# The bias of the experts' reconstruction moves from VectorE's subtraction to ScalarE's square

## The chip, the cores and the metric

One Trainium2 chip, of which the kernel uses one core. The metric is the device time of one execution in microseconds (us); lower is better. A core has five engines that run their own queues in order: TensorE (PE in the rows; its weight loads are PEld), VectorE (DVE), ScalarE (ACT), GpSimd (POOL) and SyncE (SP, here the queue that issues the DMAs). They meet through semaphores.

## The reference

A batch of 64 sequences of 128 tokens, 256 wide, goes through two layers: cross attention and a quantised feed-forward net, then cross attention and a feed-forward net with a selected adapter. The last one matters here:

```python
base = einsum('btd,do->bto', x, W_base) + b_base
h = relu(einsum('btd,edh->ebth', x, Wd1) + bd1[:, None, None, :])
recon = einsum('ebth,ehd->ebtd', h, Wd2) + bd2[:, None, None, :]
losses = mean((recon - x[None]) ** 2, axis=(2, 3))
idx = argmin(losses, axis=0)
a = relu(einsum('btd,bdr->btr', x, Wa_down[idx]) + ba_down[idx][:, None, :])
return base + einsum('btr,bro->bto', a, Wa_up[idx]) + ba_up[idx][:, None, :]
```

Each of 8 experts reconstructs the sequence; the one with the smallest squared error lends its adapter. Only the comparison of the losses is used, so their sum stands for their mean.

## The kernel before, in words

Two sequences are one pair `p`, 32 pairs in all; a pair's activations are 256 columns, `T`, held transposed with the width of 256 on partitions in two halves `k`. The work of a pair is cut into steps, and each step has a slot: the step with offset `o` runs for pair `p` at `t = o + 16 p`. Each engine has one loop over `t`, in which an order written out by hand says what it does in each slot. So steps of five pairs are interleaved on every engine, and after the fill one period of 16 slots finishes one pair. An engine that waits for a semaphore holds all that stands behind it in its loop.

The steps that the change touches or that stand around it:

- TensorE, `reconstruct(p, m)` (L1261): the reconstructions of experts 2m and 2m+1, each a PSUM bank of 512 columns (two halves of the width, 256 columns each).
- VectorE, `differences(p, e)` (L942): for each half, (reconstruction + `bd2s`) - `xT3` into the SBUF tile `dif`, 256 columns an instruction; four such tiles serve the eight experts in turn.
- ScalarE, `squares(p, e)` (L683): for each of the two sequences, the square of 2 x 128 columns with its sum into a column of `acc`. Such a call leaves two instructions in the trace, an ACTIVATE and an ACTIVATION_READ_ACCUMULATOR.
- TensorE, `losses(p)` (L1269): a matmul with ones sums `acc` over the partitions; `choose` on VectorE finds the expert, and SP's `gather` fetches its adapter.
- ScalarE, `exps(l, p, j)` (L639): the exponential of 512 columns of scores. All scores for it go through one PSUM bank, `X`: `scores_t` (L1192) may write group j+1 only when the exponential of group j is done.
- ScalarE, `copy_xT(2, p)` (L616): copies the transposed activations out of PSUM, and TensorE's `queries(1, p)` (L1154) reads the copy. `high(1, 0, p)` (L630) then takes the queries out of PSUM, `values1` (L647) the values, and `relus` (L663), the two `hd_relus` (L675) and `a_relus` (L690) are activations with a bias of one number per partition.

In ScalarE's loop the squares stand among those. In the order of one period, with the pairs left out: exps(1,1), squares 0, exps(1,2), squares 1, values1, exps(1,3), squares 2, squares 3, exps(1,4), copy_xT(2), high(1,0), exps(1,5), squares 4, exps(1,6), copy_xT(1), squares 5, squares 6, exps(1,7), squares 7, relus 0, exps(0,0). In TensorE's loop, queries(1) stands between reconstruct 2 and scores(0,3); losses stands behind mix(1,1), and behind losses come scores(0,7), count and scores_t(0,1), which needs exps(0,0) done.

Of the kernel before, what the change touches and what calls it, by code (L numbers as in the profile page):

```python
# [8 lines left out]
F32 = mybir.dt.float32  # L9
# [4 lines left out]
ALU = mybir.AluOpType  # L14
ACT = mybir.ActivationFunctionType
# [3 lines left out]
P = 128  # L19
B = 64  # L20
D = 256
KD = D // P
# [4 lines left out]
E = 8  # L27
R = 64
PB = 2
NP = B // PB  # L30
T = PB * P
# [81 lines left out]
def build(nc, x, lens, mask, mask_t, wq0, bq0, wk0, bk0, wv0, bv0, wo0, bo0, w1t, b1, w2t, b2,  # L113
          wq1, wk1, wv1, wo1, w_base, wd1, bd1, wd2, bd2, adapters, ctx_in, out):
    with ExitStack() as ctx:
        def sb(name, shape, dt):
            return ctx.enter_context(nc.sbuf_tensor(name, shape, dt))
# [4 lines left out]
        def sem(name):  # L122
            return ctx.enter_context(nc.semaphore(name))

        def signal(name, per=1):
            return Signal(sem(name), per)
# [20 lines left out]
        bd2s = sb("bd2s", [P, E, KD], F32)  # L147
        ident = sb("ident", [P, P], F32)
        onesb = sb("onesb", [P, P], BF16)
        ones = sb("ones", [P, 1], F32)  # L150
# [17 lines left out]
        xT3 = sb("xT3", [P, 2, KD, T], F32)  # L168
# [29 lines left out]
        hhl = sb("hhl", [P, 2, KF, T], F16)  # L198
        hd = sb("hd", [P, E // 2, T], F32)
        dif = sb("dif", [P, 4, KD, T], F32)  # L200
        acc = sb("acc", [P, E, PB], F32)
        lneg = sb("lneg", [1, PB, E], F32)
        lmax = sb("lmax", [1, PB, 8], F32)
        lidx = sb("lidx", [1, PB, 8], U32)
# [11 lines left out]
        bank = {name: DB[k] for name, k in place.items()}  # L216
# [19 lines left out]
        loss_ready = signal("loss_ready")  # L236
# [11 lines left out]
        squared = signal("squared", E * PB)  # L248
# [17 lines left out]
        v0_copied = signal("v0_copied")  # L266
        x_low = signal("x_low")
        h_low = signal("h_low", KF // 2)
        diffed = signal("diffed", E * KD)
        loss_out = signal("loss_out")  # L270
        best_loss = signal("best_loss", PB)
        expert_found = signal("expert_found", PB)
# [327 lines left out]
        def _(act):  # L600
# [76 lines left out]

            def squares(p, e):
                loss_ready.done(act, p - 1)
                diffed.done(act, p, 2 * e + 1)  # L680
                for b in range(PB):
                    blk = dif[:, e % 4, :, b * P:b * P + P]
                    nc.scalar.activation(blk, blk, ACT.Square, accum_out=acc[:, e, b:b + 1]).then_inc(squared.sem, 1)  # L683

            def a_relus(p):
                down_ready.done(act, p)
# [7 lines left out]
            for t in range(FIRST, END):  # L694
                for p in at(t, 64):
                    squares(p, 0)
                for p in at(t, 48):
                    exps(1, p, 2)
                for p in at(t, 65):
                    squares(p, 1)  # L700
# [3 lines left out]
                for p in at(t, 65):  # L704
                    squares(p, 2)
                    squares(p, 3)
# [71 lines left out]
        def _(dve):  # L778
# [154 lines left out]
            def differences(p, e):  # L933
                rec_ready.done(dve, p, e // 2)
                if p == 0 and e == 0:
                    dve.wait_ge(w_late, 16 * len(LATE))
                if e >= 4:
                    squared.done(dve, p, 2 * (e - 4) + 1)
                else:
                    squared.done(dve, p - 1, 2 * (e + 4) + 1)  # L940
                for k in range(KD):
                    nc.vector.scalar_tensor_tensor(  # L942
                        out=dif[:, e % 4, k], in0=bank[f"rec{e}"][:, k * T:k * T + T],
                        scalar=bd2s[:, e, k:k + 1], in1=xT3[:, p % 2, k], op0=ALU.add,
                        op1=ALU.subtract).then_inc(diffed.sem, 1)

            def choose(p):
                loss_ready.done(dve, p)
# [27 lines left out]
            for t in range(FIRST, END):  # L976
                for p in at(t, 16):
                    turn_out(0, p, 1)
                for p in at(t, 64):
                    differences(p, 1)  # L980
                for p in at(t, 16):
                    scale_out(0, p, 1)
                for p in at(t, 64):
                    differences(p, 2)
                for p in at(t, 0):
                    maximum(0, p, 0)
                for p in at(t, 65):
                    differences(p, 3)
# [110 lines left out]
        def _(pe):  # L1099
            holder = {}  # L1100

            def claim(what, consumer, p, n=None):

                if what in holder:
                    last, pair, event = holder[what]
                    last.done(pe, pair, event)
                holder[what] = (consumer, p, n)

            def dense(name, consumer, p, n=None):
                claim(place[name], consumer, p, n)  # L1110
                return bank[name]

            def warm(dst, *what):

                for _ in range(WARM.get(what, 0)):
                    nc.tensor.matmul(dst[:, 0:P], ident[:], ident[:], start=True, stop=True)
# [136 lines left out]
                ins.then_inc(hd_ready.sem, 1)  # L1253

            def reconstruct(p, m):
                dst = [dense(f"rec{2 * m + s}", diffed, p, 4 * m + 2 * s + 1) for s in range(2)]
                hd_relu.done(pe, p, m)
                for k in range(KD):
                    for s in range(2):
                        half = slice(R * s, R * s + R)  # L1260
                        ins = nc.tensor.matmul(dst[s][:, k * T:k * T + T], wd2s[half, m, k * P:k * P + P], hd[half, m],  # L1261
                                               start=True, stop=True)
                ins.then_inc(rec_ready.sem, 1)

            def losses(p):
                dst = dense("loss", loss_out, p)
                warm(dst, "losses", p)
                squared.done(pe, p)
                nc.tensor.matmul(dst[0:1, 0:E * PB], ones[:], acc[:].rearrange("p e b -> p (e b)"), start=True, stop=True)\  # L1269
                    .then_inc(loss_ready.sem, 1)  # L1270

            def down(p):
                dst = dense("down", a_relu, p)
# [22 lines left out]
            for t in range(FIRST, END):  # L1296
                for p in at(t, 64):
                    reconstruct(p, 1)
# [18 lines left out]
                for p in at(t, 67):  # L1317
                    reconstruct(p, 2)
# [12 lines left out]
                for p in at(t, 68):  # L1331
                    reconstruct(p, 3)
# [16 lines left out]
                for p in at(t, 71):  # L1349
                    losses(p)  # L1350
# [126 lines left out]
```

## Time and profile before

| | us |
|---|---|
| median of 3 runs (1646.77 to 1651.4) | 1646.82 |
| the profiled execution, its own time | 1648.25 |
| its span, which all rows below are in | 1646.4 |
| busy: TensorE matmuls | 1566.2 (95%) |
| busy: VectorE | 1307.6 (79%) |
| busy: GpSimd | 1100.4 (67%) |
| busy: ScalarE | 893.3 (54%) |

The chain of work that ended last is 80% TensorE, 7% VectorE and 1% ScalarE. A busy share is a mean over fill, steady part and end; what a change is worth has to be read in the steady part and in the end apart. In a timeline row, the first number is the start in us from the span's start, the second the time taken (of all merged instructions where there is "x8"), and brackets hold the engine's idle time before the row and what ended it.

### The profile page before, as it was taken

The numbers are of one execution on the slowest core, as the hardware profiler recorded it, in microseconds if no ns is written. First come the engines' busy times: TensorE is split into PE (matmuls) and PEld (weight loads), VectorE is DVE, ScalarE is ACT, GpSimd is POOL, SyncE is SP. The second block draws the span as 40 slices with busy tenths as digits, with TensorE's granted clock in tenths as the row PEclk, the third lists the DMA queues.
The fourth block names the chain that finished last, engine by engine and source line by source line (L and its number), as shares of the span: only waits on it lengthen the run. The fifth ranks groups of instructions, "written<-read, shape, count | busy, mean of one in ns | idle before, by whom it ended". The sixth has DMA issues, their size and how long they took to land.

```text
span 1646.4 us, 44358 instructions
## 1 busy us (share of the span) xinstructions
PE 1566.2 (95%) x15358; PEld 1303.5 (79%) x15358; DVE 1307.6 (79%) x5141; ACT 893.3 (54%) x2465; POOL 1100.4 (67%) x1197
## 2 busy tenths in 40 slices
PE   5788999999999999999999999999999999999887
PEld 4666888888888888888888888888888888887666
DVE  7457888898888888988888889888888898887552
ACT  0134565665555656655556566655565665555542
POOL 4576777766776777667777776667777766766300
PEclk7889999999999999999999999999999999999988
DMA  8446666555656665555566655565666465553311
GB/s 202 79 85 95 95 102 106 92 99 95 99 102 108 103 107 93 102 92 98 102 108 104 105 94 101 95 96 100 108 111 99 90 102 94 98 82 50 56 36 33
DMA packets 286482, 157.28 MB, mean 96 GB/s; under 512 B 39089, under 2 KB 281906, under 8 KB 286258
## 3 DMA queue, kind: packets, MB, share of 16 engines
q1 hardware_dynamic: 286258, 154.44, 54.8%
q8 instruction: 123, 2.02, 0.6%
q14 instruction: 101, 0.83, 0.2%
HBM read 111.36 MB, written 41.96 MB: 93 GB/s over the span
## 4 chain that ended last, share of the span: by engine, by line
PE 80%; DVE 7%; issue 4%; DMA 4%; POOL 3%; SPq 1%; ACT 1%; DVEq 0%; POOLq 0%; ACTq 0%
PE psD L1261 7%; PE psS L1179 7%; PE psD L1251 6%; PE psV L1206 6%; PE psD L1162 6%; PE psX L1192 6%; PE psD L1219 6%; PE psD L1154 6%; PE psD L1240 6%; PE psD L1144 6%; PE psD L1232 6%; PE psD L1288 4%; PE psD L1124 3%; DMA qs<-scr 3%; PE psD L1290 2%
## 5 line engine op out<-in xcount | busy, mean ns | idle before, releaser
L532 POOL TENSOR_TENSOR pT<-pT,keep 128x512 f32<-128x512 f32 x256 | 321.2, 1271 | 87.6 <-ACT pT L639 87.5
L639 ACT ACTIVATE pT<-psX 128x512 f32<-128x512 f32 x512 | 305.2, 596 | 110.5 <-PE psX L1192 104.8
L517 POOL TENSOR_SCALAR xn<-xr,mv,rstd 128x256 f32<-128x256 f32 x256 | 312.0, 1226 | 10.4
L491 POOL TENSOR_SCALAR veps<-mv 128x2 f32<-128x2 f32 x128 | 29.3, 229 | 355.8 <-DVE mv L811 353.5
L876 DVE CUSTOM_DVE_ANT_0 dump<-psS,bias 128x128 bf16<-128x128 f32 x1024 | 233.8, 282 | 19.8 <-PE psS L1179 18.1
L1179 PE MATMUL psS<-ks,qs 65*128 65x128 f16 x2048 | 200.6, 221 | 24.9 <-DMA qs<-scr 22.9
L942 DVE SCALAR_TENSOR_TENSOR dif<-psD,bd2s,xT 128x256 f32<-128x256 f32 x512 | 213.6, 465 | 12.8 <-PE psD L1261 12.7
L683 ACT ACTIVATE dif<-dif 128x256 f32<-128x256 f32 x512 | 207.6, 414 | 25.6 <-DVE dif L942 22.9
L1192 PE MATMUL psX<-qs,ks 67*128 67x128 f16 x2048 | 199.8, 219 | 11.3 <-ACT pT L639 10.2
L1179 PEld LDWEIGHTS psS<-ks,qs 65*128 65x128 f16 x2048 | 145.8, 98 | 73.1 <-issue 27.3
L868 DVE TENSOR_REDUCE mx<-psS 128x4 f32<-128x512 f32 x256 | 169.4, 671 | 24.2 <-PE psS L1179 24.1
L1192 PEld LDWEIGHTS psX<-qs,ks 67*128 67x128 f16 x2048 | 139.9, 97 | 45.9 <-ACT pT L639 18.8
L616 ACT ACTIVATE xT<-psD 128x512 f32<-128x512 f32 x96 | 57.2, 596 | 198.5 <-PE psD L1124 198.5
L537 POOL TENSOR_TENSOR hhl<-work,hhl 128x512 f16<-128x512 f32 x128 | 147.6, 1160 | 18.9 <-ACT hhl L669 16.1
L1206 PE MATMUL psV<-pT,v 128*32 128x128 f32 x4096 | 140.9, 279 | 10.3 <-POOL pT L532 4.6
L630 ACT ACTIVATE packed<-psD 128x512 f16<-128x512 f32 x96 | 57.4, 598 | 171.6 <-PE psD L1154 75.9
L1261 PE MATMUL psD<-hd,wd2s 64*128 64x256 f32 x1024 | 146.0, 404 | 2.6 <-DVE dif L942 2.6
L1232 PE MATMUL psD<-xs,w1q 128*128 128x256 f16 x1024 | 134.4, 274 | 1.2 <-DVE xs L924 1.2
L663 ACT ACTIVATE work<-psD,b1s 128x256 f32<-128x256 f32 x256 | 108.0, 478 | 48.1 <-PE psD L1232 43.7
L1206 PEld LDWEIGHTS psV<-pT,v 128*32 128x32 f32 x4096 | 106.1, 111 | 30.8 <-issue 12.1
L1162 PE MATMUL psD<-wv,ctxT 128*128 128x256 f32 x512 | 130.4, 399 | 0.0
L1154 PE MATMUL psD<-xT,wq 128*128 128x256 f32 x512 | 126.2, 389 | 2.1 <-ACT xT L616 2.1
(102 smaller groups left out, 3218.0 us busy)
## 6 DMA issues: line engine op xcount, KB each, us to landing
scr<-packed SPq DMA_DIRECT2D x128, 256.0 KB, 2.9
ks<-scr SPq DMA_DIRECT2D x256, 128.0 KB, 5.3
qs<-scr SPq DMA_DIRECT2D x256, 128.0 KB, 4.4
adapter<-in_adapters SPq DMA_DIRECT2D x64, 192.5 KB, 2.6
xr<-in_x SPq DMA_DIRECT2D x32, 256.0 KB, 2.8
ctxT<-in_ctx SPq DMA_DIRECT2D x32, 256.0 KB, 2.8
qs<-mrows SPq DMA_DIRECT2D x512, 2.0 KB
out_y<-xr SPq DMA_DIRECT2D x32, 256.0 KB, 5.3
```

The costliest lines, as they stand in the source:

```text
L517: nc.gpsimd.tensor_scalar(xn[:, XN[s], b], xr[:, p % NX, b], mv[:, s, b, 0:1], rstd[:, s, b:b + 1], ALU.subtract, ALU.mult).then_inc(norme ...
L532: nc.gpsimd.tensor_tensor(blk, blk, keep[:, p % 2, j // 4].unsqueeze(1).to_broadcast([P, 4, P]), ALU.mult).then_inc(masked.sem, 1)
L639: nc.scalar.activation(pT[:, j], X[:], ACT.Exp, scale=SCALE).then_inc(exp_done[l].sem, 1)
L876: ins = nc.vector.tensor_tensor_reduce(out=dump[:, a], in0=S[:, a * P:a * P + P], in1=bias0[:, p % 2, b], scale=1.0, scalar=-3e38, op0=ALU ...
L942: nc.vector.scalar_tensor_tensor(out=dif[:, e % 4, k], in0=bank[f"rec{e}"][:, k * T:k * T + T], scalar=bd2s[:, e, k:k + 1], in1=xT3[:, p % ...
L1154: ins = nc.tensor.matmul(dst[:, m * T:m * T + T], wq[l][:, k, m * P:m * P + P], src[:, k], start=(k == 0), stop=(k == KD - 1))
L1162: ins = nc.tensor.matmul(dst[:, b * D:b * D + D], ctxT[:, p % NC, k * T + b * P:k * T + b * P + P], wv[l][:, k], start=(k == 0), stop=(k = ...
L1179: ins = nc.tensor.matmul(S[:, a * P:a * P + P], qs[0:MASK_ROW + 1, r, h, t0:t0 + P], ks[0:MASK_ROW + 1, r, h, t0:t0 + P], start=True, stop ...
L1192: ins = nc.tensor.matmul(X[:, a * P:a * P + P], ks[0:ROWS, r, h, t0:t0 + P], qs[0:ROWS, r, h, t0:t0 + P], start=True, stop=True)
L1206: ins = nc.tensor.matmul(V[32 * a:32 * a + 32, n * P:n * P + P], v2[l][:, b, n // 2 * UH + 2 * a + n % 2], pT[:, 4 * b + n, a * P:a * P + ...
L1232: ins = nc.tensor.matmul(dst[:, m * T:m * T + T], w1q[:, k, f0:f0 + P], xs16[:, part, k], start=(n == 0), stop=(n == 2 * KD - 1))
L1261: ins = nc.tensor.matmul(dst[s][:, k * T:k * T + T], wd2s[half, m, k * P:k * P + P], hd[half, m], start=True, stop=True)
```

## The change

The bias leaves the subtraction. `differences` becomes one subtraction over the whole bank, 512 columns. `squares` passes the bias to the activation, which adds it before the square. As the bias differs between the two halves of the width, one activation can cover only one half: four activations of 128 columns for an expert, where there were two of 256. `acc` becomes twice as large, and `losses` sums it with two accumulating matmuls. The semaphore `diffed` counts experts rather than halves.

```diff
-        acc = sb("acc", [P, E, PB], F32)
+        acc = sb("acc", [P, KD, E, PB], F32)
@@ squares (ScalarE)
-                diffed.done(act, p, 2 * e + 1)
+                diffed.done(act, p, e)
                 for b in range(PB):
-                    blk = dif[:, e % 4, :, b * P:b * P + P]
-                    nc.scalar.activation(blk, blk, ACT.Square, accum_out=acc[:, e, b:b + 1]).then_inc(squared.sem, 1)
+                    for k in range(KD):
+                        blk = dif[:, e % 4, k, b * P:b * P + P]
+                        ins = nc.scalar.activation(blk, blk, ACT.Square, bias=bd2s[:, e, k:k + 1],
+                                                   accum_out=acc[:, k, e, b:b + 1])
+                    ins.then_inc(squared.sem, 1)
@@ differences (VectorE)
-                for k in range(KD):
-                    nc.vector.scalar_tensor_tensor(
-                        out=dif[:, e % 4, k], in0=bank[f"rec{e}"][:, k * T:k * T + T],
-                        scalar=bd2s[:, e, k:k + 1], in1=xT3[:, p % 2, k], op0=ALU.add,
-                        op1=ALU.subtract).then_inc(diffed.sem, 1)
+                nc.vector.tensor_tensor(dif[:, e % 4].rearrange("p k t -> p (k t)"), bank[f"rec{e}"][:],
+                                        xT3[:, p % 2].rearrange("p k t -> p (k t)"), ALU.subtract)\
+                    .then_inc(diffed.sem, 1)
@@ reconstruct (TensorE)
-                dst = [dense(f"rec{2 * m + s}", diffed, p, 4 * m + 2 * s + 1) for s in range(2)]
+                dst = [dense(f"rec{2 * m + s}", diffed, p, 2 * m + s) for s in range(2)]
@@ losses (TensorE)
-                nc.tensor.matmul(dst[0:1, 0:E * PB], ones[:], acc[:].rearrange("p e b -> p (e b)"), start=True, stop=True)\
-                    .then_inc(loss_ready.sem, 1)
+                for k in range(KD):
+                    ins = nc.tensor.matmul(dst[0:1, 0:E * PB], ones[:], acc[:, k].rearrange("p e b -> p (e b)"),
+                                           start=(k == 0), stop=(k == KD - 1))
+                ins.then_inc(loss_ready.sem, 1)
```

## Rows read from the trace of the kernel before

**Rows 1.** Busy time by stretch; columns: length, busy (instructions) by engine, granted clock, DMA.

```profile
600.00:1000.00 400.00, 397.96 (x4005) 331.97 (x4004) 337.54 (x1341) 233.83 (x650) 289.29 (x313) 1.00 0.60 102
```

**Rows 2.** Waits of TensorE's matmuls, 250 to 1400 us; columns: total, times, longest.

```profile
PE psS L1179 <- DMA qs<-scr: 1.1, 3, 0.4
PE psD L1219 <- DVE attT L911: 1.1, 2, 0.8
PE psD L1288 <- ACT aT L690: 0.3, 1, 0.3
```

**Rows 3.** Groups of instructions, shapes apart: busy us, mean ns, idle before.

```profile
L942 DVE SCALAR_TENSOR_TENSOR dif<-psD,bd2s,xT 128x256 f32<-128x256 f32 x512 | 213.6, 465 | 12.8 <-PE psD L1261 12.7
L965 DVE TENSOR_TENSOR xr<-psD,xr 128x512 f32<-128x512 f32 x32 | 22.1, 692 | 71.0 <-PE psD L1290 71.0
L683 ACT ACTIVATE dif<-dif 128x256 f32<-128x256 f32 x512 | 207.6, 414 | 25.6 <-DVE dif L942 22.9
L683 ACT ACTIVATION_READ_ACCUMULATOR dif<-dif 128x1 f32 x512 | 101.0, 197 | 0.0
L675 ACT ACTIVATE hd<-psD,bd1s 128x256 f32<-128x256 f32 x128 | 53.8, 471 | 113.1 <-PE psD L1251 113.1
L647 ACT ACTIVATE v<-psD 128x256 f32<-128x256 f32 x64 | 21.1, 381 | 14.2 <-PE psD L1162 14.2
L690 ACT ACTIVATE aT<-psD,adapter 64x128 f32<-64x128 f32 x64 | 23.0, 360 | 30.2 <-PE psD L1278 29.4
```

**Rows 4.** Timeline of ScalarE through one steady period, in part.

```profile
806.34 0.60 ACT L639 ACTIVATE pT<-psX 128x512 f32<-128x512 f32 x1 [1.53 <-PE psX L1192]
806.83 0.41 ACT L683 ACTIVATE dif<-dif 128x256 f32<-128x256 f32 x1
...
807.23 0.41 ACT L683 ACTIVATE dif<-dif 128x256 f32<-128x256 f32 x1
...
809.74 0.66 ACT L647 ACTIVATE v<-psD 128x256 f32<-128x256 f32 x2 [0.39 <-PE psD L1162]
...
810.28 0.60 ACT L639 ACTIVATE pT<-psX 128x512 f32<-128x512 f32 x1
...
814.02 0.60 ACT L616 ACTIVATE xT<-psD 128x512 f32<-128x512 f32 x1 [1.00 <-PE psD L1124]
...
817.01 0.60 ACT L630 ACTIVATE packed<-psD 128x512 f16<-128x512 f32 x1 [2.39 <-PE psD L1154]
...
824.91 0.84 ACT L663 ACTIVATE work<-psD,b1s 128x256 f32<-128x256 f32 x2 [1.01 <-PE psD L1232]
825.64 0.60 ACT L639 ACTIVATE pT<-psX 128x512 f32<-128x512 f32 x1
```

**Rows 5.** Timeline of TensorE through the same period, in part.

```profile
814.98 1.99 PE L1154 MATMUL psD<-xT,wq 128*128 128x256 f32 x8
...
825.93 0.20 PE L1269 MATMUL psD<-acc,ones 128*1 128x16 f32 x2
826.07 0.40 PE L1179 MATMUL psS<-ks,qs 65*128 65x128 f16 x4
...
826.41 0.39 PE L1192 MATMUL psX<-qs,ks 67*128 67x128 f16 x4
826.64 1.95 PE L1144 MATMUL psD<-ctxT,wk 128*128 128x256 f32 x8
```

**Rows 6.** Timeline of the end: pairs 29 and 30, then the last.

```profile
1556.94 0.60 ACT L639 ACTIVATE pT<-psX 128x512 f32<-128x512 f32 x1
...
1557.60 0.40 PE L1192 MATMUL psX<-qs,ks 67*128 67x128 f16 x4 [1.01 <-ACT pT L639]
1557.93 1.08 PE L1206 MATMUL psV<-pT,v 128*32 128x128 f32 x32
...
1601.83 1.94 PE L1206 MATMUL psV<-pT,v 128*32 128x128 f32 x32 [2.16 <-ACT pT L639]
...
1633.22 0.21 PE L1269 MATMUL psD<-acc,ones 128*1 128x16 f32 x2
```

More of the change, by code:

```diff
@@ L268, in build @@
         h_low = signal("h_low", KF // 2)
-        diffed = signal("diffed", E * KD)
+        diffed = signal("diffed", E)
         loss_out = signal("loss_out")
```

## The prediction, made before the changed kernel was seen

> **What bounds the kernel now.** I read the busy time by stretch first. In 400 us of the steady part TensorE's matmuls are busy for 397.96 us at a granted clock of 1.00, which is the 2.4 GHz level; VectorE is busy for 337.54 and ScalarE for 233.83 [rows 1]. Then TensorE's waits: between 250 and 1400 us there are three rows, 2.5 us together, and one of them, 0.3 us, names ScalarE [rows 2]. So TensorE sets the period (46.84 us: the exponential that starts at 806.34 comes again at 853.18). A faster VectorE is worth nothing there, and a slower ScalarE costs nothing until one of its steps comes later than TensorE wants it. The shares don't say where that is, as ScalarE's 58% is not spread evenly. The timelines of ScalarE and TensorE through one period do, laid side by side.
>
> **The subtraction.** Two instructions of 256 columns, 213.6 / 256 = 0.834 us an expert, become one of 512. The nearest row, a subtraction's twin (PSUM and SBUF in, SBUF out, f32, 512 columns), takes 0.692 us [rows 3]. VectorE gets 0.14 us an expert back, 1.1 us a period, 36 us in all. TensorE waits for it almost nowhere in the steady part [rows 2], so I count it at nothing there.
>
> **The squares.** Now an expert is two activations, 0.40 us from start to start, the read of the accumulator included [rows 4]: 0.80 us. It becomes four, of half the columns and with a bias. Half the columns: the bias activations of 256 and of 128 columns take 471 and 360 ns, so 128 columns fewer save 0.11 us. The bias: activations of 256 columns out of PSUM take 471 ns with and 381 ns without one, so it costs 0.09 us [rows 3]. Start to start that gives 0.40 - 0.11 + 0.09 = 0.38 us, 1.52 us an expert, 0.72 more than now. The bounds: if the bias hides under the instruction before it, 0.29; if nothing overlaps, as between the two activations of L690 (0.74 us for the two of them in the timeline, so 0.38 from start to start), 0.38 and about 0.09 for the read's slot, 0.47. I take 0.38, since both of its terms are differences of rows that are otherwise alike, and L690 runs on 64 partitions with another operand.
>
> The Trainium skill bears on that choice (ScalarE: Activation LUTs, What ACT_TABLE_LOAD costs): an activation with a pointer operand costs 280 ns and 0.833 ns a column, each pointer some 93 ns of it, and neighbours overlap by 93 ns. The trace's 0.09 for the bias agrees. By that rule a half would be 387 ns less the overlap, with the read's slot near 0.385, which speaks for the middle and against 0.47. The same page's rules for kernel authors would leave an add to VectorE.
>
> **Where ScalarE comes late, first place.** It starts exps(1,1) at 806.34 after waiting for TensorE. From there to copy_xT(2) it has four exponentials at 0.49 (806.34 to 806.83), values1 at 0.54 (809.74 to 810.28) and four experts' squares [rows 4]. Now that is 1.96 + 0.54 + 3.20 = 5.70, and gaps fill the rest up to 814.02. With the change it is 1.96 + 0.54 + 6.08 = 8.58 us without a gap: the copy starts at 814.92 and ends at 815.52. Release takes 0.05 (the exponential of 1556.94 ends at 1557.54, the matmul starts at 1557.60 [rows 6]). TensorE wants to start queries(1) at 814.98 [rows 5] and starts at 815.57: 0.59 us late. On the way the two-deep places hold: X for exps(1,3) is free by 811.5, wanted at 812.0.
>
> **Second place.** high(1,0) waits for the queries, so it starts at 817.01 + 0.59 = 817.60. Behind it come five activations of 512 columns at 0.49 (itself, exps(1,5), exps(1,6), copy_xT(1), exps(1,7)), four experts at 1.52, relus 0 at 0.73 (824.91 to 825.64) and exps(0,0) at 0.60 [rows 4]: 817.60 + 2.45 + 6.08 + 0.73 + 0.60 = 827.46, with the release 827.51. TensorE wants scores_t(0,1) at 826.41 [rows 5], 827.00 after the first delay: 0.51 more. After a true wait the next group follows a group of scores at 0.33 instead of 0.23 (1557.60 to 1557.93 against 826.41 to 826.64) [rows 5, 6]: 0.10. After that ScalarE waits for TensorE again several times, so nothing is carried into the next period.
>
> **The loss.** One more matmul a pair, two records: 825.93 to 826.07, 0.14 us [rows 5]. It stands just ahead of the second stall and hides in it. If that stall is absent, it costs 0.14 x 32 = 4.5 us.
>
> **The ends.** First place: pairs 0 to 29 have a queries(1) two pairs on, 30 x 0.59 = 17.7 us. Second: pairs 0 to 27 have an exps(0,0) four pairs on, 28 x 0.61 = 17.1 us. In the squares of pairs 29 and 30 little other TensorE work is left, and mix(1,1) waits for ScalarE already (2.16 us for pair 30 [rows 6]). Laying 1.52 us an expert through the same order: for pair 29 exps(1,3) ends 1.0 later, queries(1) starts 2.05 later, mix(1,1) about 3.8 later, of which 0.59 is counted: 3.2 more. For pair 30, seven experts stand ahead of exps(1,7), partly in gaps: 3.7. The last pair's eight squares now end behind the warm-up matmuls that stand ahead of the loss at 1633.22 [rows 6]: from a first square at 1621.7, 8 x 1.52 ends at 1633.9, with the second loss matmul 1.0 later. Together 7.9 us.
>
> **The sum.** 17.7 + 17.1 + 3.2 + 3.7 + 1.0 = 42.7 us on the profiled execution's own 1648.25 (span 1646.4 and 1.85 around it): 1691. The median of the runs lies 1.4 lower, so 1690. It hangs on the start-to-start time of a half: 16 halves stand ahead of each place, so 0.01 us on it is 0.32 us a period, some 10 us in all. The two places stop stalling at 0.345 (16 x 0.345 = 5.52 against 3.20 and 2.3 of slack). From 0.345 to 0.41 the time goes from about 1656 to 1720.
>
> **Rivals.** (a) ScalarE's slack covers the squares, not slower: the bias hides, a half costs 0.29 from start to start, below the 0.345 from which it decides. Then no place stalls; the loss matmul costs 2 to 4.5 us, the ends lose about 1 and get 1 back from VectorE: 1647 to 1652, 1650. For it: 54% busy. Against it: the 0.09 between two rows of one shape. (b) No overlap in such short activations: 0.47. That is 0.09 x 16 x 2 = 2.9 us a period more, 84 us, and 5 at the ends: 1780. For it: L690's pair. Against it: the squares overlap today although a read stands between them, and so do L675's two activations (0.84 for two of 471 ns). (c) VectorE turns out to pace the period, and its 1.1 us a period come back: 1647 - 36 = 1611 at most. Against it: rows 2. (d) The change doesn't do what it says: a subtraction over 512 columns isn't faster than two of 256. It would alter nothing, as long as VectorE stays off the path.
>
> **Chances.** The forecast (two stalls a period, a half between 0.345 and 0.42) 0.76, with (d) in it; (a) 0.11; (b) 0.08; (c) 0.05. A measurement of this kernel can tell 0.3%, 5 us, from no change. Faster 0.05, all of (c). Same 0.10, nearly all of (a). Slower 0.85. The range of 1656 to 1722 takes in the forecast from the point where it starts to stall to a half of 0.41, and leaves out most of (a), (b) and (c).
>
> **What would show it.** In the profile after, L683 should have 1024 activations near 0.40 us, 0.38 from start to start (two of them with their reads 0.76), and as many reads, and ScalarE should be busy for about 190 us more. TensorE's waits should have two new rows in every period: L1154 on ACT xT L616, about 30 times near 0.6 us, and L1192 on ACT pT L639, about 28 times near 0.5. The period should be 48.0 us. VectorE should lose 36 us of busy time. If the period stays 46.9, the half is cheaper than 0.345, and if it is near 51, nothing overlaps. The forecast's weakest step is the 0.38; next to it that nothing of a late period is carried over, since a third place could then stall.

## The result and the profile after

The changed kernel takes 1685.78 us (median of 4 runs, 1681.19 to 1687.65) against 1648.16 for the kernel before in the same comparison. The ratio is 1.0233, 95% interval 1.021 to 1.0256: 2.3% slower, 37.6 us. The forecast was 1690, 43 us slower, in a range of 1656 to 1722. The profiled execution after took 1687.24 us, its span is 1685.4; before, 1648.25 and 1646.4. So the two spans, on which the following rests, are 39.0 us apart. One kernel's executions scatter: 30 of the kernel before, in a later comparison, took 1641.6 to 1651.4 us, the shorter ones at a mean granted clock of 0.983 and the longer at 0.978. So a few us in a single profile can be chance.

The busy time by stretch of the kernel after, in the stretch of [rows 1] (columns as there):

```profile
600.00:1000.00 400.00, 392.65 (x3939) 326.21 (x3938) 323.60 (x1251) 272.24 (x894) 288.31 (x312) 1.00 0.58 99
```

TensorE is idle for 7.4 us in 400, where it was idle for 2.0, at the same granted clock of 1.00. The waits of its matmuls between 250 and 1400 us, which answer [rows 2], say why:

```profile
PE psD L1155 <- ACT xT L616: 13.1, 24, 0.6
PE psX L1193 <- ACT pT L639: 4.7, 24, 0.2
```

These two rows are all there is. Both are once a period, 24 times in these 24 periods: queries(1) (now L1155) waits for ScalarE's copy, and scores_t(0,1) (now L1193) for the exponential before it. The three waits of before are gone. The groups that answer [rows 3], with the square now on L684 and the subtraction on L944:

```profile
L684 ACT ACTIVATE dif<-dif,bd2s 128x128 f32<-128x128 f32 x1024 | 396.1, 396 | 1.1 <-DVE dif L944 1.0
L684 ACT ACTIVATION_READ_ACCUMULATOR dif<-dif,bd2s 128x1 f32 x1024 | 201.3, 197 | 0.0
L944 DVE TENSOR_TENSOR dif<-psD,xT 128x512 f32<-128x512 f32 x256 | 167.9, 669 | 15.8 <-PE psD L1262 12.7
```

The timeline of ScalarE at the first place, which answers the first part of [rows 4]:

```profile
818.08 0.60 ACT L639 ACTIVATE pT<-psX 128x512 f32<-128x512 f32 x1 [1.53 <-PE psX L1193]
818.57 0.39 ACT L684 ACTIVATE dif<-dif,bd2s 128x128 f32<-128x128 f32 x1
818.86 0.19 ACT L684 ACTIVATION_READ_ACCUMULATOR dif<-dif,bd2s 128x1 f32 x1
818.96 0.39 ACT L684 ACTIVATE dif<-dif,bd2s 128x128 f32<-128x128 f32 x1
...
826.21 0.59 ACT L639 ACTIVATE pT<-psX 128x512 f32<-128x512 f32 x1
826.69 0.59 ACT L616 ACTIVATE xT<-psD 128x512 f32<-128x512 f32 x1
829.36 0.60 ACT L630 ACTIVATE packed<-psD 128x512 f16<-128x512 f32 x1 [2.08 <-PE psD L1155]
```

A half takes 0.385 us from start to start (0.39 from 818.57 to 818.96, and 0.385 as the mean of the rows behind it). From exps(1,1) to the copy there is no gap left, 8.61 us where there were 7.68; behind the copy ScalarE is idle for 2 us. TensorE through the same period, which answers [rows 5]:

```profile
825.65 1.13 PE L1262 MATMUL psD<-hd,wd2s 64*128 64x256 f32 x8
827.33 1.99 PE L1155 MATMUL psD<-xT,wq 128*128 128x256 f32 x8 [0.55 <-ACT xT L616]
...
838.27 0.26 PE L1271 MATMUL psD<-acc,ones 128*1 128x16 f32 x4
838.46 0.40 PE L1180 MATMUL psS<-ks,qs 65*128 65x128 f16 x4
838.81 0.28 PE L1132 MATMUL psD<-mtb,onesb 128*128 128x256 bf16 x1
839.29 0.40 PE L1193 MATMUL psX<-qs,ks 67*128 67x128 f16 x4 [0.20 <-ACT pT L639]
839.52 1.95 PE L1145 MATMUL psD<-ctxT,wk 128*128 128x256 f32 x8
```

The reconstruction before queries(1) takes 1.07 us from start to start when nothing waits (806.23 to 807.30 in the kernel before), so queries(1) was due at 826.72 and starts 0.61 later. From queries(1) to scores_t(0,1) it is 11.96 us, and was 11.43 [rows 5]: 0.53 more. The wait's own row shows only 0.20 of it, as the groups ahead of it come later too: scores 0.19 behind the loss (0.14 before), count 0.35 behind scores (0.23 before), and scores_t 0.48 behind count (0.11 before).

The start of the loss matmul marks a period. In the following table, read from such rows of each kernel, "fill" is the time to the first loss, "26 periods" goes from there to the 27th, and "end" from there to the end of the span. "Period" is the commonest of the 26. In the changed kernel all 26 lie within 0.01 us of it, in the kernel before ten, and eight with the second loss matmul alone. The ratios are to the kernel before in the same comparison (medians of 1645.3 to 1648.2), so two kernels are compared by their ratios.

| kernel | median us | ratio to before | fill | 26 periods | period | end |
|---|---|---|---|---|---|---|
| before | 1648.2 | 1 | 215.1 | 1222.9 | 46.84 | 208.5 |
| after | 1685.8 | 1.0233 | 214.4 | 1247.7 | 47.99 | 223.3 |
| subtraction alone | 1638.3 | 0.9939 | 213.0 | 1219.1 | 46.84 | 204.4 |
| halves without bias | 1640.6 | 0.9961 | 213.8 | 1219.2 | 46.89 | 205.5 |
| bias in one half | 1648.4 | 1.0012 | 213.7 | 1219.5 | 46.88 | 212.8 |
| second loss matmul alone | 1646.0 | 0.9989 | 216.2 | 1225.5 | 46.88 | 203.0 |
| first four experts | 1661.0 | 1.0083 | 213.7 | 1234.6 | 47.49 | 210.9 |
| last four experts | 1657.9 | 1.0067 | 216.9 | 1231.1 | 47.36 | 209.8 |
| copy ahead of squares 3 | 1664.6 | 1.0107 | 216.0 | 1231.8 | 47.38 | 217.8 |
| two operands | 1788.2 | 1.0859 | 221.5 | 1332.4 | 50.93 | 235.3 |
| squares alone | 1687.7 | 1.0260 | 213.2 | 1247.6 | 47.98 | 223.4 |
| both places moved | 1697.4 | 1.0323 | 213.7 | 1260.7 | 48.4 | 217.3 |
| six of eight | 1641.4 | 0.9979 | 214.2 | 1219.9 | 46.88 | 205.6 |
| moved, end as before | 1687.5 | 1.0259 | 214.0 | 1260.1 | 48.4 | 211.8 |

The 39.0 us between the two spans are thus 24.8 in the 26 periods, 14.8 in the end, and 0.7 less in the fill.

The ends hold more than waits. The mean granted clock there is 0.93 before and 0.92 after, but 0.97 with the subtraction alone, without bias, and with the second loss matmul alone. The matmuls of the end are busy for 181.6, 185.9, 176.9, 176.8 and 176.4 us in these five. The kernel before and the one with the second loss matmul alone differ by little more than that matmul. Still their ends are 5.4 us apart, and the matmuls' busy time there 5.2: that is the clock.

### The profile page after: what moved, and what is told of

The parts are those of the page before. It is cut to its first block, busy times and chain, and to the rows that moved or that the text cites. A ratio compares the mean times of both kernels' runs of the same rounds, so it can differ in the third digit from the quotient of the medians.

```text
span 1685.4 us, 45254 instructions
## 1 busy us (share of the span) xinstructions
PE 1575.6 (93%) x15422; PEld 1304.9 (77%) x15422; DVE 1270.8 (75%) x4885; ACT 1055.4 (63%) x3489; POOL 1100.7 (65%) x1197
## 4 chain that ended last, share of the span: by engine, by line
PE 54%; ACT 33%; issue 5%; DMA 3%; POOL 2%; DVE 2%; SPq 1%; POOLq 0%; DVEq 0%; ACTq 0%
ACT dif L684 21%; PE psD L1155 7%; PE psD L1252 6%; ACT pT L639 6%; PE psD L1241 6%; PE psD L1233 4%; PE psX L1193 4%; PE psV L1207 4%; PE psD L1145 4%; PE psD L1291 4%; PE psS L1180 3%; PE psD L1220 3%; PE psD L1262 2%; PE psD L1125 2%; DMA qs<-scr 2%
## 5 line engine op out<-in xcount | busy, mean ns | idle before, releaser
L684 ACT ACTIVATE dif<-dif,bd2s 128x128 f32<-128x128 f32 x1024 | 396.1, 396 | 1.1 <-DVE dif L944 1.0
L1193 PE MATMUL psX<-qs,ks 67*128 67x128 f16 x2048 | 201.0, 220 | 24.8 <-ACT pT L639 22.1
L1180 PE MATMUL psS<-ks,qs 65*128 65x128 f16 x2048 | 199.8, 220 | 24.2 <-DMA qs<-scr 22.2
L684 ACT ACTIVATION_READ_ACCUMULATOR dif<-dif,bd2s 128x1 f32 x1024 | 201.3, 197 | 0.0
L1193 PEld LDWEIGHTS psX<-qs,ks 67*128 67x128 f16 x2048 | 137.6, 98 | 70.4 <-ACT pT L639 44.1
L871 DVE TENSOR_REDUCE mx<-psS 128x4 f32<-128x512 f32 x256 | 169.6, 671 | 24.9 <-PE psS L1180 24.8
L944 DVE TENSOR_TENSOR dif<-psD,xT 128x512 f32<-128x512 f32 x256 | 167.9, 669 | 15.8 <-PE psD L1262 12.7
L1155 PE MATMUL psD<-xT,wq 128*128 128x256 f32 x512 | 127.3, 392 | 19.3 <-ACT xT L616 19.3
```

The lines of the kernel that those rows point to most:

```text
L684: ins = nc.scalar.activation(blk, blk, ACT.Square, bias=bd2s[:, e, k:k + 1], accum_out=acc[:, k, e, b:b + 1])
L871: nc.vector.reduce_max(mx[:, l, b, half * UH + s:half * UH + s + UH - 1:2], S[:].rearrange("p (a t) -> p a t", a=4), AX.X).then_inc(max_do ...
L1155: ins = nc.tensor.matmul(dst[:, m * T:m * T + T], wq[l][:, k, m * P:m * P + P], src[:, k], start=(k == 0), stop=(k == KD - 1))
L1180: ins = nc.tensor.matmul(S[:, a * P:a * P + P], qs[0:MASK_ROW + 1, r, h, t0:t0 + P], ks[0:MASK_ROW + 1, r, h, t0:t0 + P], start=True, stop ...
L1193: ins = nc.tensor.matmul(X[:, a * P:a * P + P], ks[0:ROWS, r, h, t0:t0 + P], qs[0:ROWS, r, h, t0:t0 + P], start=True, stop=True)
```

## The experiments

The theory was: two places a period, at each of which 16 halves stand ahead of a step of ScalarE that TensorE waits for, with a threshold of 0.345 us a half; VectorE's part is worth nothing. The rivals: ScalarE's load as such, the count of instructions rather than the bias, VectorE's share in the balance.

**The subtraction alone.**

```diff
-                for k in range(KD):
-                    nc.vector.scalar_tensor_tensor(..., scalar=bd2s[:, e, k:k + 1], ...)
+                nc.vector.tensor_tensor(dif[:, e % 4] ..., bank[f"rec{e}"][:], xT3[:, p % 2] ..., ALU.subtract)
```

> The kernel before, with VectorE's part of the change alone: one subtraction of 512 columns, and the bias left out (part of the computation is missing). ScalarE keeps two squares of 256 columns, TensorE one loss matmul. VectorE saves what it saves in the changed kernel (36.8 us busy). Theory (TensorE sets the period, VectorE is off the path): within 0.3% of before, 1643 to 1651. Rival (VectorE's time comes back in part and the changed kernel's loss is larger than it looks): faster than before, down to 1612.

Measured: 1638.27, ratio 0.9939 (0.9914 to 0.9963), 8.5 us faster. The theory missed, and its rival holds in part. The usual period is the same, 46.84. But the kernel before doesn't keep it: its 26 periods are 5.0 us longer than 26 x 46.84, and with the faster subtraction they are 1.3 longer. What stands in TensorE's rows between 250 and 1400 us is now one wait:

```profile
PE psX L1190 <- DMA qs<-mrows: 0.3, 1, 0.3
```

The waits of [rows 2] for a transfer that stands behind VectorE's `low`, and for VectorE's transposed attention, are gone. In the kernel before, one such delay looks like this (in the timeline of all engines; VectorE's `scale_out`, then output(0)):

```profile
1302.56 0.42 DVE L907 TENSOR_TENSOR atok<-otok,psV 128x256 f32<-128x256 f32 x1
1303.02 0.45 DVE L911 STREAM_TRANSPOSE attT<-atok 128x256 f32<-128x256 f32 x1
...
1303.61 0.67 PE L1219 MATMUL psD<-wo,attT 128*128 128x256 f32 x2 [0.77 <-DVE attT L911]
```

The spans are 9.9 us apart: 2.1 in the fill, 3.8 in uneven periods, 4.1 in the end. VectorE's busy time fell by 42.1 us (1307.6 to 1265.5). Only the 3.8 can be laid to it by these rows, and they come again in other kernels: the 26 periods take 1219.1 to 1219.9 us in the four that relieve VectorE and don't stall (this one, without bias, bias in one half, six of eight), and 1222.9 and 1225.5 in the two that don't relieve it. The end's 4.1 go with the clock (0.93 before, 0.97 here), which was 0.97 with the second loss matmul alone too, where VectorE does its old work. The fill is as short with the squares alone (213.2), where VectorE does its old work as well. Something is left at the same clock all the same: at 0.981, two runs of this kernel took 1639.4 and 1640.4 us, and five of the kernel before 1645.8 to 1647.2. Where what the 3.8 leave of these 6 us lies was not separated.

**Four halves without the bias.**

```diff
-                        ins = nc.scalar.activation(blk, blk, ACT.Square, bias=bd2s[:, e, k:k + 1],
+                        ins = nc.scalar.activation(blk, blk, ACT.Square,
```

> The changed kernel with its four halves, but without the bias in the activation (the bias is left out of the computation). Theory: a half then takes 0.29 us from start to start, below the 0.345 at which the two places begin to stall. Both stalls are gone; the period is 46.85 and the 0.14 of the second loss matmul, 47.0; with about 1 us at the ends 1653. Rival (the count of instructions and accumulator reads costs, the bias doesn't): a half stays near 0.385 and the time near 1686.

Measured: 1640.55, ratio 0.9961 (0.9947 to 0.9975). ScalarE's timeline at the first place:

```profile
808.29 0.32 ACT L684 ACTIVATE dif<-dif 128x128 f32<-128x128 f32 x1
...
808.58 0.32 ACT L684 ACTIVATE dif<-dif 128x128 f32<-128x128 f32 x1
...
811.54 0.60 ACT L616 ACTIVATE xT<-psD 128x512 f32<-128x512 f32 x1 [0.34 <-PE psD L1125]
```

A half takes 0.29 us and the copy waits for TensorE again, not TensorE for the copy: no wait of TensorE's matmuls is left between 250 and 1400 us. This kernel leaves the bias out. Both stalls are gone, as the theory says, and the count of instructions is not what costs. The total is 12 us below what was expected: the subtraction's gain was not in the expectation, and the second loss matmul costs less.

**The bias in one half.**

```diff
-                        ins = nc.scalar.activation(blk, blk, ACT.Square, bias=bd2s[:, e, k:k + 1],
+                        ins = nc.scalar.activation(blk, blk, ACT.Square,
+                                                   **(dict(bias=bd2s[:, e, 0:1]) if k == 0 else {}),
```

> The changed kernel with the bias in the first of the two halves alone (the bias of the other half is left out of the computation): 0.385 and 0.29, mean 0.338 us a half. Theory (a threshold at 0.345): still almost no stall, period 47.0 to 47.1, 1653 to 1657. Rival (the loss is in proportion to ScalarE's added time, without a threshold): of the 33 us between no bias and both biases half, so 1669.

Measured: 1648.40, ratio 1.0012 (0.9998 to 1.0027); the period is 46.88, the same as without any bias. So the steady part has a threshold, and 0.34 a half lies below it. Of the 7.9 us above the kernel without bias, the spans show 7.3 in the end (212.8 against 205.5), where a cost appears before the steady part has any. More than half of these 7.3 is the clock: it is 0.94 there against 0.97, and the matmuls of the end are busy for 180.8 us against 176.8. This wasn't one execution: the mean clock of the ten runs is 0.978 with the bias in one half and 0.982 without it.

**The second loss matmul alone.**

```diff
-                nc.tensor.matmul(dst[0:1, 0:E * PB], ones[:], acc[:] ..., start=True, stop=True)
+                for k in range(KD):
+                    ins = nc.tensor.matmul(dst[0:1, 0:E * PB], ones[:], acc[:, k] ...,
+                                           start=(k == 0), stop=(k == KD - 1))
```

> The kernel before with the second loss matmul alone (its operand holds zeros). Theory: TensorE is saturated, so the matmul's 0.14 us a pair shows in full: 4.5 us, 1652.5. Rival: it fits in a gap of TensorE and costs nothing, within 1 us of before.

Measured: 1645.97, ratio 0.9989 (0.9974 to 1.0005), not 1.003. The theory's price was wrong, and by the time the rival holds (within 1 us). The timeline of TensorE:

```profile
828.68 0.26 PE L1272 MATMUL psD<-acc,ones 128*1 128x16 f32 x4
828.86 0.40 PE L1181 MATMUL psS<-ks,qs 65*128 65x128 f16 x4
```

Four records take 0.18 us to the next group, two took 0.14 [rows 5]: the second matmul costs 0.04 a pair, 1.3 us in all (the commonest period goes from 46.84 to 46.88). The total is too rough to show that: the 26 periods of this execution are 2.7 us longer than before, mostly by uneven ones, and its end is 5.4 shorter. The 0.14 was not a price for each matmul; most of it passes once, behind the group before.

**The change for the first four experts, and for the last four.** Both with the test `e < 4` or `e >= 4` in `squares` and `differences`:

```diff
+                    if not (e < 4):
+                        blk = dif[:, e % 4, :, b * P:b * P + P]
+                        nc.scalar.activation(blk, blk, ACT.Square, accum_out=acc[:, 0, e, b:b + 1]).then_inc(squared.sem, 1)
+                        continue
```

> The changed kernel for experts 0 to 3 alone; experts 4 to 7 are as before the change (bias added by VectorE, two squares of 256 columns). Theory: only the first place stalls (queries(1) behind copy_xT(2)), 0.6 us x 30 = 18; the second loss matmul is not hidden any more, 4; and about 3 at the ends: 1672, with no matmul wait of scores_t for the exponential in the steady part. Rival (ScalarE's total load sets the loss, wherever it lies): half of the 37.6, 1667, and waits at both places.

> The changed kernel for experts 4 to 7 alone; experts 0 to 3 are as before the change. Theory: only the second place stalls (scores_t(0,1) behind exps(0,0)), 0.53 us x 28 = 15, the loss matmul hidden in it, and about 4 at the ends: 1667, with no wait of queries(1) for the copy in the steady part. Rival (total load): waits at both places, near 1667 as well, so the waits decide between the two and not the time.

Measured: 1661.03, ratio 1.0083 (1.0056 to 1.011), and 1657.93, ratio 1.0067 (1.0041 to 1.0093). All waits of TensorE's matmuls between 250 and 1400 us, for the first four experts:

```profile
PE psD L1168 <- ACT xT L617: 13.5, 25, 0.5
```

and for the last four:

```profile
PE psX L1206 <- ACT pT L640: 4.7, 24, 0.2
```

Each half of the change makes its own stall and not the other's. Against the 46.88 of the kernel with two loss matmuls, the periods are 0.61 and 0.48 longer, 1.09 together; the whole change has 1.11. So it is not the total load that sets the period. The totals are 11 and 9 us below the expectations. Both took VectorE's saving at nothing, and the first took the loss matmul at 4 us.

**The copy ahead of squares 3.**

```diff
                     squares(p, 2)
-                    squares(p, 3)
                 for p in at(t, 50):
                     exps(1, p, 4)
                 for p in at(t, 34):
                     copy_xT(2, p)
+                for p in at(t, 66):
+                    squares(p, 3)
```

> The changed kernel with one step moved on ScalarE: squares 3 behind copy_xT(2) instead of ahead of exps(1,4). ScalarE's work is the same. Theory: the squares go into the 2 us in which ScalarE waits for queries(1) anyway, so the first stall is gone and the second stays: 18 to 20 us less than the changed kernel, 1667, period 47.4. Rival (ScalarE is simply too full, the lateness is carried on to the next step): the stall reappears elsewhere, above 1680.

Measured: 1664.57, ratio 1.0107 (1.0082 to 1.0133), 1667 expected. The work on ScalarE is unchanged and the only wait left is the second:

```profile
PE psX L1194 <- ACT pT L639: 4.8, 24, 0.2
```

The squares went into ScalarE's idle 2 us behind the copy. The rival, that ScalarE is too full, is out for the first place.

**A second operand per partition.**

```diff
-                        ins = nc.scalar.activation(blk, blk, ACT.Square, bias=bd2s[:, e, k:k + 1],
+                        ins = nc.scalar.activation(blk, blk, ACT.Square, bias=bd2s[:, e, k:k + 1], scale=ones[:, 0:1],
```

> The changed kernel with a second number per partition in each of the squares' activations, a scale of 1.0 (same values). Theory: each such operand adds 0.09 us to a half, 16 halves ahead of each of the two places, so 2 x 1.5 = 3.0 us a period more: period 51.0 and 1686 + 84 + 5 = 1775. Rival (a second operand comes with the first for free): 1686.

Measured: 1788.24, ratio 1.0859 (1.0831 to 1.0886). The period is 50.93, where 51.0 was expected. The group of the squares here, beside the one without bias (from the second experiment):

```profile
L684 ACT ACTIVATE dif<-dif,bd2s,ones 128x128 f32<-128x128 f32 x1024 | 490.7, 488 | 1.1 <-DVE dif L944 1.0
```

```profile
L684 ACT ACTIVATE dif<-dif 128x128 f32<-128x128 f32 x1024 | 301.1, 306 | 1.1 <-DVE dif L944 1.0
```

306, 396 and 488 ns with none, one and two operands: 90 and 92 ns each. The total is 13 us above the expectation; the last section tells of 8 of them.

**The squares alone, with VectorE's two instructions kept.**

```diff
+        zer = sb("zer", [P, 1], F32)
@@ differences (VectorE)
-                nc.vector.tensor_tensor(dif[:, e % 4] ..., bank[f"rec{e}"][:], xT3[:, p % 2] ..., ALU.subtract)
+                for k in range(KD):
+                    ins = nc.vector.scalar_tensor_tensor(..., scalar=zer[:, 0:1], ..., op0=ALU.add, op1=ALU.subtract)
```

> The changed kernel without VectorE's part: ScalarE adds the bias in four halves, TensorE has two loss matmuls, but VectorE keeps its two instructions of 256 columns (they add a column of zeros). Theory: where the period is paced by ScalarE's two late steps, VectorE's saving buys nothing; it counts only in the fill and at the ends (about 5 us). Period 47.99 as in the changed kernel, 1690. Rival (the two parts simply add up: the subtraction alone was worth 8.5 us): 1694 or more, with a longer or uneven period.

Measured: 1687.73, ratio 1.0260 (1.0243 to 1.0277). The period is 47.98, and of the 26 only one differs from that by more than 0.02; the end is that of the changed kernel, too (223.4), and the fill is 1.2 shorter (213.2). The spans are 1684.2 here and 1685.4 there. So in the steady part VectorE's saving is worth nothing beside the late squares. The traces show nothing of it in the fill and the end either, where 5 us were expected. The totals are less sharp: the two ratios are 0.0027 apart, some 4 us, and their intervals overlap; at the same mean clock of 0.977, one run here took 1686.0 us and two of the changed kernel 1687.2 and 1687.7.

**Both places moved, and a version that should beat both.** The first has the order of the experiment with the copy ahead of squares 3, and on top of it:

```diff
@@ ScalarE: squares 7 from ahead of relus 0 to behind exps(0,0)
@@ TensorE
+                for p in at(t, 71):
+                    losses(p)          # behind scores_t(0, p, 1), no longer behind mix(1, p, 1)
@@ VectorE: choose(p) from ahead of maximum(0, p, 7) to behind it
```

> The changed kernel with the order changed at both places: on ScalarE squares 3 behind copy_xT(2) and squares 7 behind exps(0,0), on TensorE losses behind scores_t(0,1), on VectorE choose behind maximum(0,7). The work is the same. Theory: no stall in the steady part, period 46.89, but the ends keep their loss: 1648. Rival (ScalarE's load as such): the period stays near 47.4, 1664.

Measured: 1697.37, ratio 1.0323 (1.0306 to 1.0341), slower than the change itself, where the theory had 1648 and its rival 1664. Both old waits are gone from the rows of 250 to 1400 us, and a third has come, 27.0 us in 24 times, here in the timeline of one period:

```profile
842.59 0.39 PE L1194 MATMUL psX<-qs,ks 67*128 67x128 f16 x4
...
843.76 0.20 ACT L684 ACTIVATION_READ_ACCUMULATOR dif<-dif,bd2s 128x1 f32 x1
...
844.10 0.25 PE L1272 MATMUL psD<-acc,ones 128*1 128x16 f32 x4 [1.13 <-ACT dif L684]
844.28 1.59 PEld L1146 LDWEIGHTS psD<-ctxT,wk 128*128 128x128 f32 x8
```

The next group would have started 0.23 behind scores_t, at 842.82, and starts at 844.28: 1.46 later, and 46.88 + 1.46 is 48.34 of the 48.4 of the period. I had moved the loss behind scores, count and scores_t, which is 0.57 us (826.07 to 826.64 [rows 5]). The squares it needs moved by 2.1: they start at 842.32, behind exps(0,0), and would have started at 840.24, ahead of relus 0. With the bias on VectorE again in the last three pairs, the same order gives:

> The kernel with the order changed at both places, and with the bias on VectorE again in the last three pairs. Theory: period 46.89 and the ends as before: 1640 to 1643. Rival: moving squares 7 and the loss delays the choice of the expert, and the adapter with it, and something else waits: above 1647.

Measured: 1687.47, ratio 1.0259 (1.0239 to 1.0278). The period is 48.4 again, and the end is shorter by 5.5. The expectation of 1640 to 1643 missed by 45 us. The rival's number holds (above 1647), but the step that waits is the loss matmul itself, for the squares, with the same 27.0 us in 24 times. A loss moved further back was not tried.

**Six of eight experts.**

```diff
+def wide(p, e):
+    return p < NP - 3 and e % 4 != 3
@@ squares: four halves with the bias if wide(p, e), else two squares as before the change
@@ differences: one subtraction if wide(p, e), else two with the bias as before the change
@@ losses: one matmul in the last three pairs
```

> The order of the changed kernel; the bias goes to ScalarE for six of the eight experts (not for 3 and 7), and for none in the last three pairs. Theory: three experts ahead of each place add 3 x 0.74 = 2.2 us against slacks of 2.3 and 2.4, so no stall in the steady part (period 46.89); the ends cost nothing; VectorE still saves 0.86 us a pair, of which the subtraction alone gave back 8.5 us: 1640 to 1643, faster than before. Rival (the places stall already, or the gain needs all eight): 1647 or more.

Measured: 1641.41, ratio 0.9979 (0.9968 to 0.9989): 0.2% faster than the kernel before and, by the two ratios, 2.5% faster than the changed one. The period is 46.88, and TensorE's waits between 250 and 1400 us are two, of 0.5 us together:

```profile
PE psX L1210 <- DMA qs<-mrows: 0.3, 1, 0.3
PE psS L1197 <- DMA qs<-scr: 0.2, 1, 0.2
```

Three experts' squares fit where four don't. It is the only version here that computes everything and whose interval lies below 1.

## Why the prediction held, and where it was off

**TensorE sets the period, and ScalarE costs only where it comes late: right.** The chain of work that ended last had 1% ScalarE before; after, its rows by engine and by line are:

```profile
PE 54%; ACT 33%; issue 5%; DMA 3%; POOL 2%; DVE 2%; SPq 1%; POOLq 0%; DVEq 0%; ACTq 0%
ACT dif L684 21%; PE psD L1155 7%; PE psD L1252 6%; ACT pT L639 6%; PE psD L1241 6%; PE psD L1233 4%; PE psX L1193 4%; PE psV L1207 4%; PE psD L1145 4%; PE psD L1291 4%; PE psS L1180 3%; PE psD L1220 3%; PE psD L1262 2%; PE psD L1125 2%; DMA qs<-scr 2%
```

ScalarE is busy for 63% of the span and still has idle time of 5 us in one piece, elsewhere in the period (852.74 to 857.73). Its busy time grew by 162 us (893.3 to 1055.4) where 190 was forecast; that difference was not followed up.

**The price of a half: right.** 0.38 was worked out, 0.385 measured. The bias costs 0.09, half the columns give 0.11 back (416 ns for 256 columns without a bias in the subtraction alone, 306 for 128). The rival of 0.47, from L690, is out. The estimate worked out from the Trainium skill (ScalarE: Activation LUTs, What ACT_TABLE_LOAD costs) was 0.385 us, and its 93 ns for each pointer operand stand beside 90 and 92 ns here.

**The two places: right in place and size.** 0.59 forecast and 0.61 measured, 0.61 forecast and 0.53 measured. The second was too high since the 0.10 for a group behind a true wait didn't come: scores_t to keys is 0.23 here as before (839.29 to 839.52). The period was forecast at 48.0 and is 47.99. The threshold lies between 0.338 (the bias in one half, no stall) and 0.385; three of four experts at 0.385 stay below it as well.

**VectorE's part at nothing in the steady part: right for this kernel, by the wrong reason.** Rows 2 hold 2.5 us of waits, and I left them aside. They are the mark of uneven periods that cost the kernel before 5.0 us in the 26. Less work on VectorE takes most of them away in four kernels here, and a period that is stretched for another reason does so too (squares alone). This is where most of the difference between forecast and result comes from: 26 periods at 1.15 more would be 29.9, and they are 24.8, because the reference is not 26 x 46.84. Had a half taken 0.29 us, as it does without the bias (1640.6 us), the rival that expected 1650 would have been wrong as well, on the fast side.

**The loss matmul: hidden, as said, but mis-sized.** 0.14 a pair when it shows; it is 0.04. That moved the price of rival (a).

**The ends: 14.8 where 10.9 was forecast.** The forecast is the 7.9 and the stalls of the sum that lie behind the 27th loss: the second place of pairs 26 and 27, and the first of 27, 28 and 29, 3.0 in all. The step that failed is pair 28. I counted no second place for it, as there is no exps(0,0) four pairs on. But the mix(1,1) that stands behind its squares waits for ScalarE all the same. And I let every matmul of the ends run at the same granted clock in both kernels, which they don't. The timeline of TensorE in the end, which answers [rows 6] (the mix(1,1) behind the squares of pairs 28, 29 and 30, then the last loss):

```profile
1557.03 1.93 PE L1207 MATMUL psV<-pT,v 128*32 128x128 f32 x32 [1.87 <-ACT pT L639]
...
1600.96 1.94 PE L1207 MATMUL psV<-pT,v 128*32 128x128 f32 x32 [3.25 <-ACT pT L639]
...
1639.11 1.93 PE L1207 MATMUL psV<-pT,v 128*32 128x128 f32 x32 [3.04 <-ACT pT L639]
...
1671.50 0.27 PE L1271 MATMUL psD<-acc,ones 128*1 128x16 f32 x4 [1.65 <-ACT dif L684]
```

These start 30.6, 33.3, 37.3 and 38.3 us later than before (1526.46, 1567.71, 1601.83, 1633.22). The loss of the 27th pair was 24.2 later, so it is 6.4 up to the first of them, against 2.4 in the sum. Laid against the rows of the kernel before, group by group, they are 1.8 up to and with the second place of pair 27, 1.6 in one stretch of low clock, 1.3 at the first place of pair 28 (0.59 forecast) and 1.7 at mix(1,1), forecast at nothing. The stretch of low clock, after and before, with the same instructions of TensorE behind the same wait of 1.03 us for an exponential:

```profile
1521.00:1526.00 5.00, 5.00 (x55) 3.99 (x54) 1.74 (x6) 1.88 (x4) 4.84 (x6) 0.66 0.04 7
```

```profile
1495.00:1500.00 5.00, 5.00 (x63) 4.08 (x64) 1.88 (x7) 1.91 (x4) 4.84 (x6) 1.00 0.04 7
```

From there to the second mix it is 2.7 more (3.8 forecast), to the third 4.0 (3.7), to the last loss 1.0 (1.0). Another 0.7 come behind the last loss, where the matmuls are busy for 1.0 us more at a clock of 0.86, which was 0.89.

The errors have opposite signs. The forecast puts 31.2 us into the 26 periods, 6.4 too much: 5.0 for the uneven periods of before and most of the rest for the second place. It puts 0.6 into the fill, where 0.7 went away, and 3.9 too little into the end. The forecast of 43 against 37.6 is so close partly by that luck.

## What to carry to other kernels

Work that moves to an engine with 46% idle time is free only if the idle time lies ahead of the next step that the bounding engine waits for. Add up the engine's steps between two of its waits for the bounding engine, and divide the slack by the instructions in between: that gives a threshold for one instruction, and a way to move only as many as fit (here six experts of eight). A period that is mostly constant with a few longer ones can hide a second, nearly critical engine. A saving on that one was worth 3.8 us in 26 periods here, and nothing once something else stretched the period. And before a few us of fill or end are given to a cause, compare the granted clock and the busy time of the same matmuls there.

## What was not expected of the hardware

With two operands per partition, five of the 26 periods took 1.6 us more than the other 21: the 1st, 7th, 13th, 19th and 25th. The timeline of TensorE in one of them:

```profile
526.80 0.40 PE L1193 MATMUL psX<-qs,ks 67*128 67x128 f16 x4 [0.43 <-ACT pT L639]
527.13 1.08 PE L1207 MATMUL psV<-pT,v 128*32 128x128 f32 x32
528.80 0.25 PE L1271 MATMUL psD<-acc,ones 128*1 128x16 f32 x4 [0.59 <-ACT dif L684]
...
529.91 0.61 PE L1193 MATMUL psX<-qs,ks 67*128 67x128 f16 x4 [0.20 <-ACT pT L639]
530.31 3.41 PE L1145 MATMUL psD<-ctxT,wk 128*128 128x256 f32 x8
```

Eight matmuls that take 1.95 us elsewhere take 3.41. The busy time by stretch of the same kernel shows the granted clock:

```profile
526.00:530.00 4.00, 2.73 (x51) 1.71 (x49) 2.17 (x18) 4.00 (x15) 0.07 (x1) 0.98 0.75 72
530.00:534.00 4.00, 4.00 (x17) 3.28 (x17) 3.86 (x19) 1.33 (x4) 2.67 (x3) 0.59 0.41 93
```

The clock falls for about 3 us to its 1.2 GHz level (0.59 over a stretch of 4 us that has both levels) and is back at 2.4 GHz after. In the 4 us before it fell, TensorE was busy for 2.73. But that is not what sets these periods apart. The same 8 us of the next period, counted from its loss:

```profile
578.58:582.58 4.00, 2.73 (x51) 1.70 (x49) 2.17 (x18) 4.00 (x15) 0.07 (x1) 1.00 0.86 76
582.58:586.58 4.00, 4.00 (x35) 3.57 (x35) 3.86 (x19) 2.97 (x8) 3.38 (x4) 1.00 0.35 81
```

All 26 periods have the 2.73 there, the next one with the same three waits (0.43, 0.59 and 0.20 us), and only every sixth loses the clock. What picks it no run here shows. It costs these five 8 us together, on top of the stalls.

In the changed kernel, whose stalls are 0.6 and 0.5 us, the clock is 1.00 in the whole steady part. In its end it is not, as said above: the 223.3 us there have 0.92, and the same work without the bias has 0.97, in an end that is 17.8 us shorter. The matmuls are busy for 9.1 us of these 17.8. So where ScalarE holds TensorE up in the end, the price is the waits and a slower clock behind them, about half each. Against the kernel before, whose own end has 0.93, it is 4.3 of 14.8.
